# Second pass of a layer-norm, state-scan and Fourier kernel: y products on two halves of the TensorE array, and x loaded in halves

## The reference, cut to what matters

```
xn    = layernorm(x) * gamma + beta
delta = sigmoid(xn @ w_delta + b_delta)        # 16 per token
b     = xn @ w_in + b_in                       # 16 per token
gate  = sigmoid(xn @ w_gate + b_gate)          # 512 per token
h_t   = tanh((h_{t-1} * delta_t) @ A + b_t)    # 16 states, one token after the other
y     = h @ C                                  # 16 states to 512 numbers
x1    = layernorm(x + (y * gate + x))
out   = layernorm(x1 + real(ifft(fft(x1) @ w)) + bias)
```

## Time and profile before

| | before |
|---|---|
| median of 3 runs | 904.74 us (904.02 to 906.34) |
| the profiled execution | 903.86 us |
| its span in the trace | 901.9 us |
| TensorE busy | 872.3 us (97%) |
| VectorE, ScalarE, GpSimd busy | 722.0, 566.4, 553.2 us |
| mean traffic of the transfers | 233 GB/s |
| chain of waits that ended last: share of TensorE | 88% |

### The profile page before, as it was taken

One profiled execution on the slowest core, in us unless ns is written; L12 is line 12 of the kernel. 1 busy time (PEld: TensorE's weight loads), 2 busy tenths in 40 slices (PEclk: granted clock), 3 DMA queues, 4 the chain that ended last, 5 costly groups with the idle time before them and its releaser, 6 DMA issues.

```text
span 901.9 us, 18386 instructions
## 1 busy us (share of the span) xinstructions
PE 872.3 (97%) x5306; PEld 470.3 (52%) x5306; DVE 722.0 (80%) x1510; ACT 566.4 (63%) x1063; POOL 553.2 (61%) x890
## 2 busy tenths in 40 slices
PE   7879999999999999999989999999999999999996
PEld 5334454545545545457764555555555555555553
DVE  5978888888888888876678888888888888888883
ACT  3337444444444444475554888888888888888887
POOL 2645666666666666651127687777777777877782
PEclk9999999999999999999999999999999999999999
DMA  8496777777777777637025566776687677667743
GB/s 300 166 355 252 280 274 266 273 267 270 270 267 270 267 275 272 228 107 275 2 54 176 206 219 239 270 245 224 235 273 231 229 238 257 230 236 254 248 172 140
DMA packets 94524, 209.96 MB, mean 233 GB/s; under 512 B 3616, under 2 KB 5920, under 8 KB 90528
## 3 DMA queue, kind: packets, MB, share of 16 engines
q1 hardware_dynamic: 94208, 209.41, 66.9%
q10 hardware_dynamic: 288, 0.21, 0.2%
HBM read 140.53 MB, written 67.11 MB: 230 GB/s over the span
## 4 chain that ended last, share of the span: by engine, by line
PE 88%; DVE 6%; ACT 3%; issue 2%; DMA 1%; POOL 0%; DVEq 0%; POOLq 0%; ACTq 0%
PE bank L1352 23%; PE bank L1353 23%; PE bank L1355 23%; PE bank L1342 6%; PE bank L1518 3%; PE bank L1409 2%; PE bank L1388 1%; DMA h_sb<-x_turned 1%; PE bank L1391 1%; PE bank L1469 1%; PE bank L1462 1%; PE bank L1304 1%; DVE bn L1008 1%; DVE h_lo L1198 1%; DVE xs_sb L1040 1%
## 5 line engine op out<-in xcount | busy, mean ns | idle before, releaser
L717 POOL TENSOR_TENSOR lo_sb<-xs_sb,hi_sb 128x512 f16<-128x512 f32 x128 | 149.6, 1169 | 147.3 <-ACT hi_sb L497 147.3
L760 POOL TENSOR_TENSOR x_sb<-x_sb,gate_sb 128x512 f32<-128x512 f32 x128 | 164.3, 1284 | 81.0 <-DMA x_sb<-x 63.2
L497 ACT ACTIVATE hi_sb<-xs_sb 128x512 f16<-128x512 f32 x128 | 80.6, 630 | 209.4 <-DVE xs_sb L1040 209.4
L1352 PE MATMUL bank<-wg_hi,hi_sb 128*128 128x512 f16 x512 | 194.9, 381 | 10.6 <-POOL wg_lo L722 5.2
L1353 PE MATMUL bank<-wg_lo,hi_sb 128*128 128x512 f16 x512 | 195.3, 381 | 0.0
L1352 PE MATMUL bank<-z_sb,hi_sb 128*128 128x512 f16 x512 | 194.0, 379 | 0.1
L1353 PE MATMUL bank<-z_sb,hi_sb 128*128 128x512 f16 x512 | 194.0, 379 | 0.0
L1045 DVE SCALAR_TENSOR_TENSOR lo_sb<-bank,hi_sb 128x512 f16<-128x512 f32 x128 | 88.5, 692 | 71.9 <-ACT hi_sb L643 71.4
L1355 PE MATMUL bank<-wg_hi,lo_sb 128*128 128x512 f16 x512 | 132.2, 381 | 0.0
L1355 PE MATMUL bank<-z_sb,lo_sb 128*128 128x512 f16 x512 | 131.4, 379 | 0.0
L643 ACT ACTIVATE hi_sb<-bank 128x512 f16<-128x512 f32 x128 | 76.2, 595 | 61.3 <-PE bank L1342 61.1
(11 more groups left out here) (189 smaller groups left out, 1368.8 us busy)
## 6 DMA issues: line engine op xcount, KB each, us to landing
x_sb<-x SPq DMA_DIRECT2D x63, 1024.0 KB, 6.2
gate_dram<-gate_sb SPq DMA_DIRECT2D x32, 1024.0 KB, 5.3
gate_sb<-gate_dram SPq DMA_DIRECT2D x32, 1024.0 KB, 6.7
out<-out_sb SPq DMA_DIRECT2D x31, 1024.0 KB, 5.3
h_sb<-x_turned SPq DMA_DIRECT2D x16, 1024.0 KB, 7.1
norm_sb<-x_turned SPq DMA_DIRECT2D x15, 1024.0 KB, 6.6
h_rep<-fourier_constants SPq DMA_DIRECT2D x2, 514.0 KB, 11.3
x_sb<-x SPq DMA_DIRECT2D x2, 512.0 KB, 6.1
```

What stands on the lines that cost most here:

```text
L717: pool.tensor_tensor(lo_sb[:, k % 4], xs_sb[:, k % 2], hi_sb[:, k % 4], ALU.subtract).then_inc(s_lo, 1)
L760: pool.tensor_tensor(x_sb[:, k // 4, k % 4], x_sb[:, k // 4, k % 4], gate_sb[:, k // 4, k % 4], ALU.add).then_inc(s_v, 1)
L1352: nc.tensor.matmul(dst, hi_sb[:, slot_of, t], w_hi[:, t], start=(t == 0), stop=False)
```

## The change

The y products are made in pairs. In every second slot (k even) `pair_states_out` issues two matmuls, for tiles n + 6 and n + 7. Each uses only the 64 rows of its own sequence, the first on partitions 0 to 63, the second on 64 to 127 of the array, into the two banks. The operand of C then needs no zeros, and one `c_parts` serves both; VectorE prepares it in two steps instead of four. y is now made in the same slot in which the first of the pair is gated.

To have the two sequences of a tile pair on partitions 0 to 63 and 64 to 127, `replicate_states` copies 16 partitions at a time: 32 transfers instead of 16. A new buffer `h_now` holds the states of the octet at hand; a new transfer, once a quad, copies them from `h_rep` to `h_now` at the head of `second_pass`.

The load of x is cut in two, with semaphores of their own. The first half (two tiles) is now issued after `b_normalise` of the quad's second tile, ahead of the store; the second as before. `residual` waits for x once for two tiles.

```diff
@@ SP
+            def load_half(v, q, h):
+                b = slice(2 * h, 2 * h + 2)
+                sp.dma_start(x_sb[:, q, b], x_v[v, q][:, b]).then_inc(s_bx[q][h], 16)
+
             def second_pass(v, q):
                 sp.wait_ge(s_v, v * 8 + 4 * q + 4)
+                if isinstance(v, int):
+                    for r in (2 * q, 2 * q + 1):
+                        sp.wait_ge(s_hrep[r], 8 * 16)
+                sp.dma_start(h_now[:, 2 * q:2 * q + 2],
+                             h_rep[:, 2 * q:2 * q + 2, bass.ts(v + 1, P)]).then_inc(s_hnow[q], 16)
                 load_gate(v + 1, q)
+                sp.wait_ge(s_bnorm, v * 8 + 4 * q + 2)
+                load_half(v + 1, q, 0)
                 if not isinstance(v, int):
                     store_result(v - 1, q)
                 sp.wait_ge(s_bnorm, v * 8 + 4 * q + 4)
-                load_x(v + 1, q, s_bx)
+                load_half(v + 1, q, 1)
 
             def replicate_states(done):
-                for r in range(BATCH // 2):
+                for b in range(BATCH):
                     for seg in range(4):
                         src = (h_hi, h_hi, h_lo, h_lo)[seg]
-                        sp.dma_start(h_rep[32 * seg:32 * seg + 32, r, P:SEQ],
-                                     src[32 * r:32 * r + 32, P:SEQ]).then_inc(done[r], 16)
+                        row = P // 2 * (b % 2) + STATE * seg
+                        sp.dma_start(h_rep[row:row + STATE, b // 2, P:SEQ],
+                                     src[STATE * b:STATE * b + STATE, P:SEQ]).then_inc(done[b // 2], 16)
@@ GpSimd
             def residual(n, k, v):
                 pool.wait_ge(s_gy, n + 1)
-                if k % 4 == 0:
-                    pool.wait_ge(s_bx[k // 4], v * 16 + 16)
+                if k % 2 == 0:
+                    pool.wait_ge(s_bx[k // 4][k % 4 // 2], v * 16 + 16)
@@ VectorE
             def beside_step(k):
                 if k in combined_beside:
                     combine(combined_beside[k])
-                if k in (2, 4, 6, 8):
-                    c_parts_of((k - 2) // 4, (k // 2 + 1) % 2)
+                if k in (2, 4):
+                    c_parts_of((k - 2) // 2)
@@ TensorE
-            def states_out(n, k, v):
-                if isinstance(n, int) and n < 16 and n % 2 == 0:
-                    pe.wait_ge(s_hrep[k // 2], 4 * 16)
-                if before(n, 2):
-                    pe.wait_ge(s_gy, n - 1)
-                nc.tensor.matmul(ps_y[k % 2][:], h_rep[:, k // 2, bass.ts(v, P)], c_parts[:, k % 2],
-                                 start=True, stop=True).then_inc(s_y, 1)
+            def pair_states_out(n, k, v):
+                if k % 4 == 0:
+                    pe.wait_ge(s_hnow[k // 4], v * 16)
+                pe.wait_ge(s_gy, n)
+                for j in range(2):
+                    rows = slice(P // 2 * j, P // 2 * j + P // 2)
+                    nc.tensor.matmul(ps_y[j][:], h_now[rows, k // 2], c_parts[rows],
+                                     start=True, stop=True).then_inc(s_y, 1)
@@
-                elif exists(n + 7):
-                    states_out(n + 7, (k + 7) % 8, v if k < 1 else v + 1)
+                elif k % 2 == 0 and exists(n + 6):
+                    pair_states_out(n + 6, (k + 6) % 8, v if k < 2 else v + 1)
```

More of the change, by code:

```diff
@@ L40 @@
 C_PARTS = 2 * P
-C_WIDTH = C_PARTS + 4
+C_WIDTH = C_PARTS + 2
 W_GAMMA, W_BETA, W_BIAS = 0, KT, 2 * KT
@@ L133, in build @@
         c_hi, c_lo = sb("c_hi", [P, D], F16), sb("c_lo", [P, D], F16)
-        c_parts = sb("c_parts", [P, 2, D], F16)
+        c_parts = sb("c_parts", [P, D], F16)
         c_max = sb("c_max", [P, 1])
@@ L149, in build @@
         h_rep = sb("h_rep", [P, BATCH // 2, SEQ], F16)
+        h_now = sb("h_now", [P, BATCH // 2, P], F16)
         hd = sb("hd", [P, LANES])
@@ L319, in build @@
         s_split = sem("scan_split")
-        s_bx = [sem(f"b_x_loaded{i}") for i in range(2)]
+        s_bx = [[sem(f"b_x_loaded{q}{h}") for h in range(2)] for q in range(2)]
         s_bg = [sem(f"b_gate_loaded{i}") for i in range(2)]
         s_bst = [sem(f"b_stored{i}") for i in range(2)]
+        s_hnow = [sem(f"b_states_loaded{i}") for i in range(2)]
         s_y = sem("b_y")
@@ L449, in _ @@
             for q in range(2):
-                load_x(0, q, s_bx)
+                for h in range(2):
+                    load_half(0, q, h)
                 load_gate(0, q)
@@ L458, in _ @@
                 for r in range(BATCH // 2):
-                    sp.wait_ge(s_hrep[r], 4 * 16)
+                    sp.wait_ge(s_hrep[r], 8 * 16)
                 sp.wait_ge(s_final, 1)
                 replicate_states(s_hrep2)
+                for r in range(BATCH // 2):
+                    sp.wait_ge(s_hrep2[r], 8 * 16)
             second_pass(0, 0)
@@ L616, in _ @@
                 for r in range(BATCH // 2):
-                    act.wait_ge(s_hrep[r], 4 * 16)
+                    act.wait_ge(s_hrep[r], 8 * 16)
                 with act.Fori(2, LANES) as r:
@@ L919, in split_c, with c_parts_of @@
                 nc.vector.sem_inc(s_c_split, 1)
-            def c_parts_of(j, low):
-                column = C_PARTS + 2 * j + low
-                mask = cst[:, column:column + 1]
+            def c_parts_of(low):
+                mask = cst[:, C_PARTS + low:C_PARTS + low + 1]
                 if not low:
-                    wait_own(nc.vector.tensor_scalar(c_parts[:, j], c_hi[:], mask, None, ALU.mult))
+                    wait_own(nc.vector.tensor_scalar(c_parts[:], c_hi[:], mask, None, ALU.mult))
                 else:
-                    nc.vector.scalar_tensor_tensor(c_parts[:, j], c_lo[:], mask, c_parts[:, j], ALU.mult,
-                                                   ALU.add)
+                    wait_own(nc.vector.scalar_tensor_tensor(c_parts[:], c_lo[:], mask, c_parts[:], ALU.mult,
+                                                            ALU.add))
             def largest_bias():
@@ L1216, in _ @@
                 for r in range(BATCH // 2):
-                    dve.wait_ge(s_hrep[r], 4 * 16)
+                    dve.wait_ge(s_hrep[r], 8 * 16)
                 dve.wait_ge(s_seen, 1)
@@ L1496, in _ @@
                 for r in range(BATCH // 2):
-                    pe.wait_ge(s_hrep2[r], 4 * 16)
+                    pe.wait_ge(s_hrep2[r], 8 * 16)
             pe.wait_ge(s_split, 1)
@@ L1554, in shape_constants @@
     row = np.arange(P)
-    for j in range(2):
-        for low in range(2):
-            c[:, C_PARTS + 2 * j + low] = (row // STATE % 2 == j) & (row // 32 % 2 == low)
+    for low in range(2):
+        c[:, C_PARTS + low] = row // STATE % 2 == low
     return c
```

## The result

| | before | changed |
|---|---|---|
| median of 15 runs each | 903.88 us | 907.36 us |
| lowest to highest | 902.13 to 906.34 | 906.39 to 912.15 |
| ratio, 95% interval | | 1.0053 (1.0040 to 1.0067) |
| profiled execution | 903.86 us, span 901.9 | 912.15 us, span 910.1 |

The change makes the kernel 0.4% to 0.7% slower, 3.5 us between the medians, where 4.2 us less and 900.5 were forecast. The profiled execution of the changed kernel is the slowest of its 15, so I compare stretches of it, not its end, and what it shows of a loss that happens once can be more than the median holds.

The account below looks back on a forecast made before the run. TensorE's list of matmuls was taken to bound pass B. Pairs -4.9, start of pass B +1.0 and scan -0.3 sum to -4.2 us on 903.86, or 899.7; with medians 0.9 higher, 900.5 us, range 893 to 912.

Parts of the forecast that it names:

- What bounds the kernel: Pass B lasts as long as TensorE's list of matmuls; the other engines have time free there.
- Pairs of y products: Pass B: 60 pairs on array halves at 0.35 us each instead of 0.43, gaining 0.08 us a pair, -4.9 us.
- rival 1: Array empties fully at each change around a pair: 0.57 us a pair, 914 us; chance of over 907 us 0.22.
- The start of pass B: SP issues 32 copies instead of 16 ahead of the second octet's gate load: +1.0 us, ends 0 and 4.4.
- x in halves: Pass B: earlier first half removes GpSimd's wait, frees nothing on TensorE, 0 us, but covers x when slots get shorter.
- h_now: One more 64 KB transfer a quad ahead of the gate load, with about four slots of room: 0 us in the loop.
- The other engines at the faster pace: Pass B's tightest wait, `ffn(n)` on `ffn_sum(n - 2)`, has 0.56 us to spare, shrinks by 0.08 and holds: 0 us.
- The scan: VectorE prepares `c_parts` in two steps instead of four; between 0 and 0.73 us saved, taken as -0.3 us.
- The sum: -4.9 + 1.0 - 0.3 = -4.2 us on the profiled 903.86 us, giving 899.7 us and a forecast median of 900.5.
- rival 3: Array changes around pairs cost 0.07 to 0.11 us each way: 902 to 907 us, about no change; chance 0.25.

Follow-up runs that it names:

- early_gate: Changed kernel with the gate load, h_now copy and first half of x for the second octet issued after 16 of 32 copies; 901.26 us, ratio 0.9976 to before.
- pairs_full_array: early_gate with each y product of a pair on all 128 rows again, zeros on the other sequence's rows; 904.02 us, ratio 1.0007 to the kernel before.
- quads: early_gate with four y products together in every fourth slot, on halves 0, 1, 0, 1; 898.52 us, ratio 0.9945 to the kernel before.
- split_copies: Kernel before with each of the 16 copies to h_rep cut into two of 16 partitions, nothing else; 906.81 us against 902.81, ratio 1.0047.
- halves_of_x_only: Kernel before with only x loaded in halves, the first one earlier; no pairs, no h_now, 16 copies; 901.83 us against 902.99, ratio 0.9993.
- quads_swapped: quads with VectorE's ffn_sum(n - 1) ahead of gated(n + 6) in each slot; 894.29 us, ratio 0.9892 to the kernel before.
- whole_x: early_gate with x loaded whole again, 1 MB a quad, behind the store; 907.93 us, ratio 1.0038 to the kernel before.

## Why the prediction was wrong, point by point

- **What bounds the kernel**: right. In each kernel without stops pass B lasted as long as TensorE's list.
- **Pairs of y products** (-4.9 us forecast): this step failed; it was worth -0.2 us (60 pairs, 6.482 against 6.485 us for two slots; 0.2 us between early_gate and pairs_full_array). The two halves overlap better than I took (under 0.01 us instead of 0.028), but the two changes cost 0.09 and 0.11 us where I had 0.035 and 0.07, so a slot with the pair takes 3.45 us instead of 3.38. The mistake is in how I read the earlier trace rows. The next full matmul started 0.09 us after a matmul that streamed one column; that is already the price, since nothing else ran. I subtracted 0.028 us of ordinary distance, which would have been hidden behind a stream of 512 columns. Then I halved the result for the way in, because the transposes seemed to leave room. They don't: the pair starts at 665.22 and the record of the transposes ends at 665.29; the next product starts at 665.54 and the pair's record ends at 665.61; in the earlier trace rows it was 465.97 and 466.04. All three are 0.07 us ahead of the record's end (the profile models these ends). So a change costs the 0.163 us on the way out less 0.07, or 0.093, in both directions. In quads the last record ahead of the way out is 0.01 us shorter, and so is the distance (0.31 instead of 0.32); that speaks for a wait until the array is nearly empty and against a fixed price. That is just the point that rival 1 named as the one from which the gain is gone.
- The rule of the Trainium skill, "TensorEngine Tiling (Array Packing)", Tiling Modes, that a change of mode drains TensorE, holds here but for those 0.07 us; I gave it too little weight. "TensorE: Matmul & The Clock Gate", Part 3, on halves that run at the same time, agrees with the trace: the two products of a pair start under 0.01 us apart.
- **The start of pass B** (+1.0 us, ends 0 and 4.4): the mechanism was right and the size wrong, since I took the issue of half a copy to be shorter. It is not (0.59 us median for 120 KB and for 60 KB). By the medians split_copies puts it at +4.0 us, and the changed kernel against early_gate, each by its own kernel before, at 3.5 + 1.5 = 5.0; the changed kernel's trace, of its slowest execution, has 6.7. The case that I took as the upper end is what happened: the gate landed 28.9 us after `n_differ`, as 494.7 for 465.85 says. Two things were missing in its 4.4 us: `h_now` stands between the copies and TensorE and was late itself, so that the two stops together are 5.4 us; and behind the second stop TensorE ran at 1.2 GHz for a while, 1.4 us more. The landing of the gate was not slower than elsewhere (5.9 us, 5.8 for the same load before). The two halves of x, issued right behind it, were (6.6 and 7.5 us, 4.1 in the median of that kernel); GpSimd waited for them until 498.5, but the y of tile 8 was gated only at 497.88.
- **x in halves** (0 us): right for the kernel before (halves_of_x_only). In the changed kernels it is a cover, as the prediction said. Without it pass B of early_gate loses 7.5 us, 4.3 of them once at the start, where the place of the load may have a part; at the pace of quads_swapped it loses 9.2 us, 6.9 of them spread over the quads.
- **h_now** (0 us in the loop): right in the loop, wrong at the start.
- **The other engines at the faster pace** (0 us): right for pairs. The same wait, 0.56 us of room, became the bound with groups of four.
- **The scan** (-0.3 us): 52.23 to 51.89, -0.34. Right, and the same in other traces: 51.8 to 51.9 us with two steps, 52.2 in split_copies and halves_of_x_only, which have four. The stretch behind it became 0.55 us shorter, which the sum had not; the cause is open.
- **The sum**: the pairs missed by 4.7 us and the start by 4 to 6. Either alone would have taken most of the forecast gain; together they turned its sign.
- **The rivals**: the steady part went as rival 3. That the median landed at its upper end is luck: the start cost several times the +1.0 that rival had in it. The median lies in the stated range; its sign was forecast wrong.

## What to carry to other kernels

An overlap on parts of the array is worth the streams it saves less one emptying of the array on the way in and one on the way out, so put as many small matmuls as banks allow between two changes; here the two emptyings cost 0.21 us together, two products broke even and four gained 7 us of pass B. When a copy is cut into smaller ones, count issues on the queue and ask which load stands behind them, above all where one stage hands over to the next. The price of a rare event is read as the whole distance that it makes, before subtracting what would be hidden in another place.

## What the runs showed that I had not expected

- A change between the full array and halves costs 0.09 to 0.11 us each way, and no weight load runs ahead across it; between one pair on halves and the next it is under 0.01 us.
- Issuing a copy takes 0.6 us whether it moves 60 or 120 KB, while the loads of x take 0.37 us in the median at 512 KB and at 1 MB.
- A stop of TensorE of 2.5 us can be followed by some 3 us at 1.2 GHz, which cost 1.4 us in the changed kernel and 1.7 in whole_x. It need not be: the stop of 2.7 us at 489.8 in the changed kernel and the one of 2.15 us in split_copies were followed by matmuls 0.216 us apart.
- Waits of up to 0.16 us hide in the matmuls' records: the count of matmuls in a stretch told more than the busy time.
